# Products that share one PSUM bank move into the two rings of score banks

## The reference, cut to what matters

```python
# x: (16, 512, 128); both layers have 16 heads of 8 columns
xn = layernorm(x)
x  = x + attention_0(xn) + channel_mix(xn)     # causal; q and k: 8 normed columns and 64 linear ones
xn = layernorm(x)
x  = x + attention_1(xn) + gelu_ffn(xn)        # not causal; bias log(exp(-|pos_i - pos_j|) + 1e-8)

attention:    softmax(q k^T / sqrt(8) [+ mask or bias]) v, then a projection
channel_mix:  sigmoid(xr W_r) * (square(relu(xk W_k)) W_v)
gelu_ffn:     gelu(xn W1) W2,  W1 and W2 composed once from 32 weighted low-rank terms
```

## Time and profile before

| | |
|---|---|
| median of 3 runs | 2006.25 us (1997.91 to 2010.62) |
| the profiled execution | 2012.44 us; its span 2010.7 us |
| PE busy | 1716.7 us, 85% of the span |
| DVE busy | 1461.2 us, 73% |
| ACT busy | 1315.7 us, 65% |
| POOL busy | 925.6 us, 46% |
| mean granted clock of PE | 0.921 |

### The profile page before, as it was taken

The page is one execution under the profiler, slowest core; times in us unless marked ns, Lnnn a source line. Parts: engine busy times, 40 slices in busy tenths (PEclk is TensorE's granted clock), DMA queues, the critical chain, the costliest instruction groups (busy, mean ns, idle before and its releaser), DMA issues.

```text
span 2010.7 us, 33441 instructions
## 1 busy us (share of the span) xinstructions
PE 1716.7 (85%) x11850; PEld 667.3 (33%) x11850; DVE 1461.2 (73%) x2975; ACT 1315.7 (65%) x2518; POOL 925.6 (46%) x1144
## 2 busy tenths in 40 slices
PE   5798889888888888887689989999989999998986
PEld 2443333333333333333123323333323333233332
DVE  4457777776767767766267888888888888888882
ACT  1236666666666666655437777777777777877775
POOL 2114454443445444443213554555554555544555
PEclk9769998997989989887669999999999999999998
DMA  7222222221222122210411222212222212222200
GB/s 245 52 48 65 64 65 55 67 56 54 58 55 62 56 59 64 60 59 17 81 32 41 64 49 54 59 46 52 61 52 54 57 44 55 56 57 54 53 19 16
DMA packets 133125, 116.41 MB, mean 58 GB/s; under 512 B 16856, under 2 KB 125664, under 8 KB 132960
## 3 DMA queue, kind: packets, MB, share of 16 engines
q1 hardware_dynamic: 126272, 100.64, 21.1%
q0 software_dynamic: 4096, 8.40, 1.3%
q10 hardware_dynamic: 2592, 5.24, 0.8%
HBM read 79.63 MB, written 33.55 MB: 56 GB/s over the span
## 4 chain that ended last, share of the span: by engine, by line
PE 54%; DVE 21%; ACT 9%; issue 6%; POOL 6%; DMA 2%; SPq 2%; DVEq 0%; POOLq 0%; ACTq 0%
PE pv_acc L582 15%; PE scores_transposed L598 12%; ACT probs L877 4%; DVE maxs L1104 4%; PE work L726 4%; PE work L676 3%; DVE maxs L1099 3%; PE work L698 3%; PE scores_for_max L619 3%; PE work L648 2%; POOL x_between_layers L1163 2%; PE scores_for_max L623 2%; ACT accS L884 2%; PE scores_for_max L635 1%; DMA stacks<-parts_scratch 1%
## 5 line engine op out<-in xcount | busy, mean ns | idle before, releaser
L877 ACT ACTIVATE probs<-scores_transposed 128x512 f32<-128x512 f32 x1664 | 926.7, 600 | 322.6 <-PE scores_transposed L598 292.2
L1104 DVE TENSOR_REDUCE maxs<-scores_for_max 128x1 f32<-128x512 f32 x1024 | 653.4, 683 | 149.8 <-PE scores_for_max L619 136.6
L598 PE MATMUL scores_transposed<-stacks 62*128 62x512 bf16 (+3 forms) x2048 | 597.2, 354 | 20.6 <-ACT probs L877 15.9
L582 PE MATMUL pv_acc<-probs,vals 128*32 128x512 f32 (+3 forms) x4096 | 483.6, 546 | 91.2 <-ACT accS L884 42.7
L1241 POOL TENSOR_TENSOR probs<-probs,near_bias 128x512 f32<-128x512 f32 x256 | 330.2, 1293 | 430.9 <-ACT probs L877 430.5
L619 PE MATMUL scores_for_max<-stacks 60*128 60x512 bf16 x1024 | 351.4, 392 | 27.8 <-DVE maxs L1104 18.5
L598 PEld LDWEIGHTS scores_transposed<-stacks 62*128 62x128 bf16 x2048 | 154.7, 95 | 622.6 <-ACT probs L877 294.5
L623 PE MATMUL scores_for_max<-stacks 60*128 60x512 bf16 (+3 forms) x1024 | 269.2, 325 | 34.5 <-DVE maxs L1099 20.6
L1099 DVE TENSOR_REDUCE maxs<-scores_for_max 128x1 f32<-128x512 f32 x256 | 174.6, 682 | 106.6 <-PE scores_for_max L635 94.4
L1095 DVE TENSOR_REDUCE maxs<-scores_for_max 128x1 f32<-128x384 f32 x256 | 141.4, 552 | 134.0 <-PE scores_for_max L635 132.1
L1215 POOL TENSOR_SCALAR_AFFINE_SELECT probs<-probs 128x512 f32<-128x512 f32 x256 | 166.6, 670 | 135.8 <-ACT probs L877 135.6
(11 more groups left out here) (128 smaller groups left out, 2067.6 us busy)
## 6 DMA issues: line engine op xcount, KB each, us to landing
stacks<-parts_scratch SPq DMA_DIRECT2D x768, 64.0 KB
parts_scratch<-parts SPq DMA_DIRECT2D x64, 384.0 KB, 3.3
x_tile<-in_L_attn_x_dram SPq DMA_DIRECT2D x16, 256.0 KB, 2.8
probs<-in_fc_B_dram ACTq DMA_DIRECT2D x1, 4096.0 KB, 19.9
stage_a<-in_fc_A_T_dram SPq DMA_DIRECT2D x1, 4096.0 KB, 16.5
stacks<-mT SPq DMA_DIRECT2D x256, 4.0 KB
x_res<-in_L_attn_x_dram SPq DMA_DIRECT2D x16, 256.0 KB, 3.5
x_tile<-x_between_layers SPq DMA_DIRECT2D x16, 256.0 KB
```

What stands on the lines that cost most here:

```text
L582: last = mm(acc[32 * j:32 * j + 32, q0:T], vals[:, B.parity(off), kt, G * pu + j, :], probs[:, row, column:column + width], start=(kt == 0 ...
L598: last = mm(st[:, bank, column:column + T - q0], ks[p][rows, h, P * kt:P * kt + P], qs[p][rows, h, q0:T], start=True, stop=True)
L877: fn(probs[:, row, :], st[:, B.packs(layer, u, number) % ST_BANKS, :], ACT.Exp, scale=SCALE).then_inc(s["exp_done"], 1)
L1104: v.reduce_max(maxs[:, su % 2, column:column + 1], s1[:, B.packs(1, su, m, so) % MAX_BANKS, :], AX_X).then_inc(s["red_done"], 1)
```

## The change

The bank `work` is gone. `scores_for_max` gets it and has four banks; `scores_transposed` keeps three. A product now takes its turn in one of the two rings: in that of `scores_for_max` if DVE reads it out last (OT0-3, FV, QT, KT, PR), in that of `scores_transposed` if ACT does (all others). A table, made once, walks all slots and gives each tile and product its bank and the use whose reading it must wait for: the fourth back in DVE's ring, the third back in ACT's. Y, one product of 4 x 128 columns, becomes four (Y0 to Y3), each with its own bank and its own copy of 128 columns by ACT. The readers' slots move: MT0-3 are read in their own slot in both layers, H3 and KT of layer 1 and FR one slot earlier, Tanh and what follows it in the feed-forward of layer 1 one slot later; ACT's copy to `accS` moves from behind the Exp at j = 1 of the last block to ahead of the Exp at j = 0. The composition of W1 and W2 in the setup uses the bank `pv_acc` instead of two banks of `scores_transposed`. What is computed stays the same.

```diff
-ST_BANKS, MAX_BANKS = 3, 3
+ST_BANKS, MAX_BANKS = 3, 4
 WORK_USES = {
-    0: {"OT0": (1, 0, -1), "MT0": (4, 0, 0), "FR": (6, 1, 1), "FK": (8, 0, 1), "FV": (13, 0, 1),
-        "OT1": (16, 0, -1), "XT": (19, 0, 2), "MT1": (20, 0, 0), "PJ0": (22, 0, 2), "PJ1": (24, 1, 2),
-        "PJ2": (28, 0, 2), "PJ3": (31, 0, 2), "OT2": (34, 0, 0), "MT2": (37, 2, 0), "FT": (40, 0, 1),
-        "QT": (46, 0, 2), "OT3": (49, 0, 0), "KT": (51, 0, 2), "MT3": (57, 1, 1)},
-    1: {"OT0": (0, 0, -1), "H0": (3, 0, 1), "MT0": (4, 2, 0), "H1": (9, 0, 1), "H2": (15, 0, 1),
-        "MT1": (17, 0, 0), "OT1": (18, 0, -1), "XT": (20, 0, 2), "H3": (24, 1, 1), "AT": (28, 0, -1),
-        "PR": (30, 0, -1), "VP": (32, 0, 1), "MT2": (34, 1, 0), "OT2": (36, 0, 0), "QT": (39, 0, 2),
-        "KT": (44, 1, 2), "OT3": (49, 0, 0), "MT3": (53, 1, 1), "Y": (57, 5, 1)},
+    0: {"OT0": (1, 0, -1), "MT0": (4, 0, 0), "FR": (6, 0, 1), "FK": (8, 0, 1), "FV": (13, 0, 1),
+        "OT1": (16, 0, -1), "XT": (19, 0, 2), "MT1": (20, 0, 0), "PJ0": (22, 0, 2), "PJ1": (24, 0, 2),
+        "PJ2": (28, 0, 2), "PJ3": (31, 0, 2), "OT2": (34, 0, 0), "MT2": (37, 0, 0), "FT": (40, 0, 1),
+        "QT": (46, 1, 2), "OT3": (49, 0, 0), "KT": (51, 1, 2), "MT3": (57, 0, 1)},
+    1: {"OT0": (0, 0, -1), "H0": (3, 0, 1), "MT0": (4, 0, 0), "H1": (9, 0, 1), "H2": (15, 0, 1),
+        "MT1": (17, 0, 0), "OT1": (18, 0, -1), "XT": (20, 0, 2), "H3": (24, 0, 1), "AT": (28, 0, -1),
+        "PR": (30, 0, -1), "VP": (32, 0, 1), "MT2": (34, 0, 0), "OT2": (36, 0, 0), "QT": (39, 1, 2),
+        "KT": (44, 1, 2), "OT3": (49, 0, 0), "MT3": (53, 0, 1),
+        "Y0": (57, 0, 1), "Y1": (58, 0, 1), "Y2": (59, 0, 1), "Y3": (60, 0, 1)},
 }
+BY_DVE = ("OT0", "OT1", "OT2", "OT3", "FV", "QT", "KT", "PR")
...
+def ring_uses():
+    uses, counts = {}, collections.Counter()
+    rings, banks = ([], []), (ST_BANKS, MAX_BANKS)
+    def add(key, ring, layer, semaphore, full=None):
+        counts[layer, semaphore] += 1
+        at = len(rings[ring])
+        before = rings[ring][at - banks[ring]] if at >= banks[ring] else None
+        taken = (layer, semaphore, counts[layer, semaphore])
+        rings[ring].append(taken)
+        uses[key] = Use(ring, at % banks[ring], before, full, taken[1:])
+    for body, slot in slots_in_order():
+        ...
+        if tile == pack[0]:
+            if body.has(0):
+                add((layer, body.number, ("st", u, number)), 0, layer, "exp_done")
+            if body.has(so):
+                add((layer, body.number + so, ("max", su, number)), 1, layer, "red_done")
+        for name, (at, later, off) in WORK_USES[layer].items():
+            if at == slot and body.has(off):
+                counts[layer, "full"] += 1
+                ring = int(name in BY_DVE)
+                add((layer, body.number, name), ring, layer, ("act_taken", "dve_taken")[ring], counts[layer, "full"])
+    return uses
...
-                def claim(name):
-                    wait(pe, s["work_taken"], B.use(name))
-                    if B.beside:
-                        wait(pe, S[B.beside.layer]["work_taken"], B.other_layers_uses(name))
+                def claim(key):
+                    use = B.use(key) if isinstance(key, str) else key
+                    if use.before:
+                        layer_, semaphore, count = use.before
+                        pe.wait_ge(S[layer_][semaphore], count)
+                    return (st, s1)[use.ring][:, use.bank, :]
...
                     for side, name in enumerate(("QT", "KT")):          # ACT
-                        if B.out(name, slot):
+                        if B.due(name, slot):
                             first_part(side)
-                        if B.out(name, slot, 2):
+                        if B.out(name, slot, 1):
                             second_part(side)
...
-                            if B.out(f"H{f}", slot, 2):
+                            if B.out(f"H{f}", slot, 3):
                                 act.wait_ge(s["gelu"], B.count(NF, f + 1, 1))
                                 fn(fc[:], fb[:], ACT.Tanh, scale=GELU_C).then_inc(s["tanh_done"], 1)
...
                     for kt in range(NT):
                         for j in range(G):
+                            eo, eu = (-1, NG - 1) if u == 0 else (0, u - 1)
+                            if j == 0 and kt == NT - 1 and B.has(eo):
+                                act.wait_ge(s["pv_done"], B.count(NG * NT, NT * eu + NT, eo))
+                                if B.has(-1 if u < 2 else 0):
+                                    filled(f"OT{u}")
+                                fn(accS[:], acc[:], ACT.Copy).then_inc(s["acc_taken"], 1)
                             number, pack, tile = TILES[layer][4 * kt + j]
                             if B.has(0) and tile == pack[-1]:
...
-                            if j == 1 and kt == NT - 1 and B.has(eo):
-                                ...
-                                fn(accS[:], acc[:], ACT.Copy).then_inc(s["acc_taken"], 1)
...
-                            if B.out(f"H{f}", slot, 3):                 # DVE
+                            if B.out(f"H{f}", slot, 4):
                                 gelu_outer(f)
```

More of the change, by code:

```diff
@@ L124 @@
 }
-USES = [sorted(((n, use[2]) for n, use in WORK_USES[layer].items()), key=lambda n: WORK_USES[layer][n[0]][0])
-        for layer in range(2)]
 def bf16_parts(x):
@@ L206, in packs, with use @@
         return EXPS[layer] * (NG * (self.number + off) + u) + number
-    def use(self, name):
-        table = USES[self.layer]
-        before = sum(1 for n in range(FIRST, self.number) for _, off in table if 0 <= n + off < NB)
-        for n, off in table:
-            if n == name:
-                break
-            before += self.has(off)
-        return before if self.i is None else self.i * (2 * len(table)) + before
-    def other_layers_uses(self, name):
-        other = self.beside
-        slot = WORK_USES[self.layer][name][0] + (other.layer == 0)
-        table = USES[other.layer]
-        before = sum(1 for n in range(FIRST, other.number) for _, off in table if 0 <= n + off < NB)
-        return before + sum(1 for n, off in table if WORK_USES[other.layer][n][0] < slot and other.has(off))
+    def use(self, key):
+        return USES[self.layer, self.number, key]
@@ new lines, with slots_in_order @@
+Use = collections.namedtuple("Use", "ring bank before full taken")
+def slots_in_order():
+    for n in range(FIRST, LAST - 1):
+        yield from ((Body(0, n), slot) for slot in range(NG * NT * G))
+    for n in range(2):
+        for slot in range(NG * NT * G):
+            yield Body(0, LAST - 1 + n), slot
+            yield Body(1, FIRST + n), slot
+    for n in range(FIRST + 2, LAST + 1):
+        yield from ((Body(1, n), slot) for slot in range(NG * NT * G))
+def ring_uses():
[9 more added lines that the diff above has]
+    for body, slot in slots_in_order():
+        layer, u, i = body.layer, slot // (NT * G), slot % (NT * G)
+        number, pack, tile = TILES[layer][i]
+        so, su = (0, u + 2) if u < 2 else (1, u - 2)
+        if tile == pack[0]:
[9 more added lines that the diff above has]
+    return uses
@@ L990, in other @@
                     if B.out(f"OT{u}", slot):
-                        filled(f"OT{u}")
-                        heads = work[:].rearrange("p (t j c) -> p t j c", t=NT, j=G)
+                        work = filled(f"OT{u}")
+                        heads = work.rearrange("p (t j c) -> p t j c", t=NT, j=G)
+                        first = Body(layer, B.number - 1).use("OT3") if u == 0 and B.has(-1) else None
+                        before = B.use(f"OT{u - 1}") if u and B.has((-1, -1, -1, 0)[u]) else first
+                        if before:
+                            dve.wait_ge(taken, before.taken[1])
                         link(v.reciprocal(rsum[:], heads[:, :, :, HD]), "rec", NG, ou + 1, oo)
@@ L1118, in _ @@
             run_both_layers(body, 0)
-            dve.wait_ge(S[0]["work_taken"], Body(0, LAST).use("OT0"))
             run_both_layers(body, 1)
```

184 lines of the change are left out of this document (89 added, 95 removed).

## The result

The changed kernel takes **2028.02 us** (median of 4 runs, 2018.61 to 2032.51) against 2006.45 us for the kernel before, measured beside it (1997.91 to 2010.62): ratio 1.0107, 95% interval 1.0056 to 1.0158. I had forecast 1981 us, between 1948 and 2025. So both the sign and the range were wrong. The profiled execution took 2032.51 us, 20.1 us more than that of before.

A forecast was written before the change was run, and what follows sets the result against it. Layer 1 was taken as PE-bound with DVE close behind, layer 0 as losing to waits and clock. Terms -34.5 + 0 + 10 - 0.5 = -25 us from 2012.4 gave 1987, the median 6 lower: 1981 us, range 1948 to 2025.

The forecast's parts named there:

- Layer 1, the copy: Copy to accS in layer 1: PE's waits at slots 48 and 0 go, 1.1 us a batch gained after 0.45 given back.
- Layer 1, slots 4 to 17, XT, H3 and PR: Layer 1: 0.7 us a batch gained at slots 4 to 17, and 0.5 us at XT, H3 and PR.
- QT in the ring: Layer 1: QT and KT hold a bank of DVE's ring until DVE's read; four banks cover it, no cost.
- The clock in layer 1: Layer 1's clock was full before the change; the sum priced no fall there.
- my rival for "slower": Clock falls at slots 42 and 6 of layer 0 and 14 to 17 of layer 1: +34 us, 2040 us; chance 0.18.
- Layer 0: Layer 0: waits sum to 0 a batch; more but cheaper clock falls cost 10 us more than now.
- The wait at slot 42: Layer 0: pack 7 waits 2.1 us for pack 5's Exp, with clock falls in nearly every batch; QT loses 0.3 us.
- PJ3: Layer 0: PJ3 takes the bank of pack 8 and waits for its Exp, 0.45 us a batch lost.
- the idle time of MT0: Layer 0: MT0's 1.36 us wait for OT0 moves to slot 6, with nothing gained.
- The passage: The passage with both layers: left at 0.
- Setup and Y: Setup saves one copy, under 1 us (0.5 in the sum); Y's three more copies on ACT are hidden.
- the second rival: DVE and ACT bound the kernel; removed waits return at slots 6, 15 and 42: no change, 2008 us; chance 0.27.

The follow-up runs named there:

- experiment 2: The changed kernel with the copy to accS put back behind the Exp at j = 1: 2027.32 us, ratio 1.0105 against the kernel before.
- experiment 1: The kernel before with only the copy to accS moved ahead of the Exp at j = 0: 2006.52 us, ratio 1.0033.
- experiment 5: Copy to accS ahead of the Exp except at layer 1's slots 12 and 28: on the kernel before 1969.86 us, on a_ft 1958.93 us.
- experiment 6: a_ft with layer 1's H2 and H3 also in the ring of four, still read by ACT: 1965.51 us, ratio 0.9838.
- experiment 8: a_ft with layer 1's accS copy late at slots 12, 28, H2, H3 in DVE's ring, QT read at 39: 1951.98 us; plus old Tanh delays, 1963.81 us.
- a_tanh: The changed kernel with layer 1's Tanh and outer product a slot earlier, as before, and H3 read a slot later: 2017.31 us, ratio 1.0061.
- a_ft: The changed kernel with layer 0's product FT in the ring of four, though ACT still reads it: 1978.52 us, ratio 0.9867.
- b_acc: Same run as experiment 1: the kernel before with only the copy to accS moved ahead of the Exp, 2006.52 us.
- b_mix: From experiment 5: the kernel before with the accS copy early in layer 0 and, in layer 1, only at slots 44 and 60: 1969.86 us, ratio 0.9859.
- a_acc: Same run as experiment 2: the changed kernel with the copy to accS back behind the Exp at j = 1, 2027.32 us.

## Why the prediction was wrong, point by point

**Layer 1, the copy (forecast: 1.1 us a batch gained; measured: none in the changed kernel, a loss of 1.1 us on the kernel before).** The waits of the earlier trace rows went away as said, at slots 48 and 0. But the same line serves four slots of the batch, and I read only the two at which PE waited. At slots 12 and 28 nobody waited for the copy, yet it stands ahead of an Exp, and at slot 28 ahead of `attT`. This was the step that failed: "Two Exps of 0.6 us that stood ahead of the copy now stand behind it, so both waits go", with 0.45 us given back. The runs put the give-back at all of it in the changed kernel (experiment 2) and at 1.2 us without the clock, 2.7 with it, on the kernel before (experiment 1, against the 1.6 us of the two waits); the gain of the right half is 1.35 and 1.45 us a batch (experiment 5), so that size was near.

**Layer 1, slots 4 to 17, XT, H3 and PR (forecast: 1.2 us; measured: -0.2).** The gains are there: blocks 8, 16 and 20 are 0.73, 0.53 and 0.69 us shorter, 1.9 us in all. They are spent in the blocks between: 12 is 1.4 us longer, 24 by 0.85. The wait before H2, which I named in a rival and among the signs but priced at nothing in the sum, comes once a batch, with another just ahead of it. PE of the changed kernel:

```profile
1304.03 0.39 PE L631 MATMUL scores_transposed<-stacks 62*128 62x512 bf16 x1 [0.41 <-DVE maxs L1139]
1305.99 0.39 PE L631 MATMUL scores_transposed<-stacks 62*128 62x512 bf16 x1 [0.59 <-ACT probs L916]
1306.98 1.13 PE L731 MATMUL scores_transposed<-xnT,w 128*128 128x512 f32 x2 [0.60 <-ACT probs L916]
...
1318.20 0.39 PE L631 MATMUL scores_transposed<-stacks 62*128 62x512 bf16 x1 [0.64 <-ACT fa L870]
1321.77 0.39 PE L631 MATMUL scores_transposed<-stacks 62*128 62x512 bf16 x1 [0.96 <-ACT probs L916]
```

Putting H2 and H3 into the other ring takes 0.88 us out of the batch with the copy early everywhere (experiment 6), and nothing where the copies at slots 12 and 28 are late (experiment 8). The -0.2 is the change of blocks 8 to 27 together (19.88 to 20.22 us), less 0.2 us that the copy at slot 12 costs (5.49 and 3.36 against 5.00 and 3.67 in blocks 12 and 16).

**QT in the ring (forecast: nothing, "four banks cover it"; measured: 0.60 us a batch lost).** Block 40, 2.52 to 3.12 us. DVE reads QT at slot 40, as before, behind the maximum of that slot. But the tile of slot 43 is the fourth behind QT in the ring, and PE gets to it 0.3 us too soon (3.7 us in 13 waits), which is half of the loss; where the other half arises was not traced. With DVE's read at slot 39 the block is 2.45 us (experiment 8).

**The clock in layer 1 (forecast: no fall; measured: falls in five of twelve batches).** The start of `attT` in three batches running, and H2 in the last of them at half speed (2.08 us, where 1306.98 above has 1.13):

```profile
1260.78 0.60 ACT L876 ACTIVATE attT<-scores_transposed 128x512 f32<-128x512 f32 x1
1321.60 0.60 ACT L876 ACTIVATE attT<-scores_transposed 128x512 f32<-128x512 f32 x1
1383.93 0.60 ACT L876 ACTIVATE attT<-scores_transposed 128x512 f32<-128x512 f32 x1
```

```profile
1367.81 2.08 PE L731 MATMUL scores_transposed<-xnT,w 128*128 128x512 f32 x2 [0.61 <-ACT probs L916]
```

60.82 us without a fall and 62.33 us with one: 1.5 us each. That is the mechanism of my rival for "slower" ("the Exp of slot 13, which H2's bank now waits for"), with its size of 1.6 us, though in five batches and not in all. a_tanh, where the Tanh comes a slot sooner, has none.

**Layer 0 (forecast: +10 us; measured: +20.6).** The wait at slot 42 came as predicted: 1.95 us where 2.1 was expected, in all 14 batches, with a fall behind each. PE also waits less at QT for it, as predicted: 7.8 us in 14 waits against 9.0. In slots 32 to 58 the mean batch lost 1.30 us (18.81 to 20.11), 18 us in all. Idle time makes 0.5 us of it, where the sum had 0.3; the clock makes 0.8, where it had 10/14 = 0.7. A fall costs 20.11 us less the 2.69 us of idle time less the 15.10 us that the stretch needs without either (17.60 - 2.50), so 2.3 us: the price that I took. So this part, forecast at 14 us, was right in mechanism and nearly in size.

What was missed is the rest of the batch, from slot 58 on to slot 32. There the sum had a gain of 0.3 us a batch (0.75 for `accS` less 0.45 for PJ3), 4 us, and the trace has a loss of 0.15 us (34.79 to 34.94), 2 us. The waits for `accS` are gone, but the idle time of MT0, moved to slot 6 as said, grew from 19.4 to 24.6 us, and the clock falls behind slot 6 in 13 of 14 batches, where it did in five before. No term of the sum had that fall. What each of them was worth no run tells, and all of this half is within the variation of layer 0.

How the idle time of slot 42 travels can be seen in the batch of the timeline. DVE, for which QT waits, had itself waited for PE before it came to the scaling of `big`. DVE of the changed kernel:

```profile
270.90 0.69 DVE L1125 TENSOR_REDUCE maxs<-scores_for_max 128x2 f32<-128x512 f32 x1 [0.64 <-PE scores_for_max L668]
271.51 1.50 DVE L1077 TENSOR_TENSOR big<-big,rrms 128x1024 f32<-128x1024 f32 x1
```

So here a wait of PE comes back as one of DVE and then again as one of PE, 1.28 us. In half of the batches the clock has fallen before PE gets to QT, and the wait is 0.24 us.

The Trainium skill ("TensorE: Matmul & The Clock Gate", "A second HAM failure mode: psum-queue depth-cycling") has PE swing between its two clocks when matmuls cycle through PSUM banks, by brief idle times between groups. The rows agree that short idle times go ahead of a fall (1.95 and 1.28 us here). They do not make the cycling itself the cause: a_ft cycles through the same seven banks and has clock 1.00 in that stretch in 11 of 14 batches.

**The passage (forecast: 0; measured: -14.7 us).** The only term that erred to the other side. In its middle the clock was 0.60 before, from 950 to 1050 us, and in the changed kernel it is 0.88 and then 0.57. b_acc and b_mix, with the old banks, have 260.8 and 255.2 us there and a_acc, with the old order, 266.6, against 279.4 before and 264.7 after; all eleven other profiles lie between 251 and 268. So either part of the change may give it, or the one trace of the kernel before has a long passage by chance. It is open.

**Setup and Y.** The time to the third `rrms` is 2.1 us longer, not 0.5 shorter; but it lies between 150.5 and 159.3 us over the twelve profiles, so nothing can be read from that. Y in four pieces costs nothing, as predicted: block 56 is 5.44 us in both.

**The sum.** Layer 1 is 46.5 us worse than forecast (+12.0 for -34.5), layer 0 10.6, the setup 2.6, the passage 14.7 better: 45 us, from 1987 to 2032. The rival that came true in part was the clock's, to which I gave 0.18, with its slot right and its layer 1 too heavy; the point from which I said it decides was not reached. What made "slower" was that the gains of layer 1 came back within the same batch, as the second rival said.

## What to carry to other kernels

When products share rings with the main loop's tiles, list for each slot which earlier use its bank waits for, and look for the reader that comes late (here ACT behind two table loads): the ring for a product should be chosen by who is *late* at that slot, not by who reads it; one choice was worth some 48 us. When an instruction is moved in a loop, price it at every slot that it serves, also where nobody waited for it, since it delays what stands behind it. A product that is read late holds its bank, and can cost time even in the longer ring (0.6 us a batch for QT). And two edits that each gain alone need not add up: moving H2 and H3 gave 0.88 us a batch with the copies early and nothing with two of them late.

## What the runs showed of the hardware

In layer 0 an idle time of 1.95 us, with another of 0.24 to 1.28 us behind it, went with a fall of PE from 2.4 to 1.2 GHz in all 14 batches; before the change the 1.47 us at slot 39 did so in five of 14 batches and not in the other nine; with the longest at 0.53 us (a_ft) the clock stayed full in 11 of 14. In layer 1 three idle times of 0.41, 0.59 and 0.60 us did it in some batches and not in others, with the same waits to within 0.01 us (1364.85, 1366.81, 1367.81 with a fall; 1304.03, 1305.99, 1306.98 without).

DVE's product of two tensors in SBUF is slowed beside POOL. In the changed kernel it usually takes 0.68 us, but here it took 1.65, while POOL added `bproj` to `x_res`; Tanh, the copy and the Exp of slot 28 stand behind it, and PE's 0.96 us at 1321.77 is the end of that chain.

```profile
1318.43 1.65 DVE L1102 SCALAR_TENSOR_TENSOR fb<-fa,fd 128x512 f32<-128x512 f32 x1
```

```profile
1318.25 1.28 POOL L1233 TENSOR_TENSOR x_res<-x_res,bproj 128x512 f32<-128x512 f32 x1
```

How long it takes goes by how much of it lies beside POOL's add: before the change the two meet for 0.2 us and it takes 0.7 us, in a_tanh for 0.3 us and it takes 0.87 us, here for 1.1 us; DVE's maxima, which read PSUM, take 0.67 to 0.69 us beside the same adds. The longest such product in layer 1 took 0.82 us before the change and 1.80 us after. The Trainium skill ("GPSIMD Engine Reference", "1. Specifications") says that both engines share interfaces to SBUF and contend when DVE reads two inputs there; the trace agrees. So moving H3 and Tanh also moved them onto POOL's adds, which no count of banks shows.
